# Rows of maxima copied by ScalarE's own queue, experts' weights loaded in pieces, down weights loaded two steps sooner

## The reference

```python
q = decoder_feature @ Wq.T                     # decoder_feature = layernorm(x)
k = encoder_feature @ Wk.T                     # encoder_feature = ctx_1024
v = encoder_feature @ Wv.T
att = softmax(einsum('bhtd,bhnd->bhtn', q, k) * scale, axis=-1)   # 2 * HEADS score maps
att = att[:, :, 0] - lam * att[:, :, 1]
x = x + einsum('bhtn,bhnd->bhtd', att, v)
...
scores = sigmoid(x @ gate_w.T); topk_w, topk_idx = top_k(scores, 2)
x = x + shared(x) + routed(x)                  # routed: silu(x @ gate) * (x @ up) @ down of 2 experts
```

## Time and profile before

| | |
|---|---|
| median of 3 runs | 2147.44 us (2145.28 to 2149.7) |
| the profiled execution | 2141.56 us; its span 2139.8 us |
| PE busy | 1966.6 us (92%) |
| VectorE, ScalarE, GpSimd busy | 1614.5 (75%), 1465.2 (68%), 1442.7 us (67%) |
| DMA | 432 MB, 202 GB/s over the span |
| chain that ended last | PE 58%, DMA 12%, SPq 10%, issue 8%, DVE 7% |

### The profile page before, as it was taken

One profiled execution on the slowest core, in us unless ns is written; L12 is line 12 of the kernel. 1 busy time (PEld: TensorE's weight loads), 2 busy tenths in 40 slices (PEclk: granted clock), 3 DMA queues, 4 the chain that ended last, 5 costly groups with the idle time before them and its releaser, 6 DMA issues.

```text
span 2139.8 us, 76271 instructions
## 1 busy us (share of the span) xinstructions
PE 1966.6 (92%) x20840; PEld 1417.8 (66%) x20840; DVE 1614.5 (75%) x4623; ACT 1465.2 (68%) x3511; POOL 1442.7 (67%) x2183
## 2 busy tenths in 40 slices
PE   3889999999999999999999999999888699999997
PEld 3556666666666666666666666666554599989996
DVE  2677878878878888788888787887776577767775
ACT  2577877777877778778787777787666355545553
POOL 4356767777777777777777676776655466666665
PEclk8899999999999999999999999999998699999999
DMA  4776666666666666667667666666764488868885
GB/s 125 201 205 193 189 185 204 192 191 196 199 194 195 195 195 196 194 199 198 192 198 199 183 189 194 196 198 187 210 206 174 146 263 263 260 199 275 258 268 171
DMA packets 606680, 432.00 MB, mean 202 GB/s; under 512 B 437571, under 2 KB 552394, under 8 KB 606160
## 3 DMA queue, kind: packets, MB, share of 16 engines
q1 hardware_dynamic: 545712, 319.34, 53.9%
q0 software_dynamic: 32256, 84.47, 10.8%
q10 hardware_dynamic: 28576, 26.55, 4.1%
HBM read 234.59 MB, written 197.72 MB: 202 GB/s over the span
## 4 chain that ended last, share of the span: by engine, by line
PE 58%; DMA 12%; SPq 10%; issue 8%; DVE 7%; POOL 3%; ACT 1%; DVEq 0%; POOLq 0%; ACTq 0%
PE mx_ps L491 9%; DMA stacks<-mxT 8%; PE o_ps L524 7%; SPq L369 6%; PE ms_ps L552 6%; PE ms_ps L752 5%; PE ms_ps L553 3%; PE ms_ps L554 3%; PE mx_ps L552 3%; PE mx_ps L554 3%; PE mx_ps L553 3%; PE ms_ps L573 3%; PE st_ps L730 3%; PE o_ps L535 3%; DVE mx L956 2%
## 5 line engine op out<-in xcount | busy, mean ns | idle before, releaser
L956 DVE TENSOR_REDUCE mx<-mx_ps 128x4 f32<-128x512 f32 x1024 | 696.0, 687 | 235.7 <-PE mx_ps L491 232.2
L800 ACT ACTIVATE prob<-st_ps 128x512 f32<-128x512 f32 x1024 | 607.6, 596 | 320.9 <-PE st_ps L484 306.6
L491 PE MATMUL mx_ps<-stacks 48*128 48x128 bf16 x4096 | 398.1, 221 | 88.9 <-DMA stacks<-mxT 67.1
L484 PE MATMUL st_ps<-stacks 50*128 50x128 bf16 x4096 | 396.7, 221 | 0.0
L491 PEld LDWEIGHTS mx_ps<-stacks 48*128 48x128 bf16 x4096 | 232.8, 95 | 244.3 <-issue 138.3
L524 PE MATMUL o_ps<-prob,v_sb 128*32 128x256 f32 x4096 | 332.0, 396 | 0.9 <-ACT oT L787 0.4
L1308 POOL DMA_INDIRECT rows_dram<-rowt,posi x256 | 255.0, 996 | 73.6 <-issue 63.6
L552 PE MATMUL ms_ps<-e_lo 128*128 128x256 f32 x768 | 269.6, 351 | 18.6 <-DVE rowt L1055 7.9
L484 PEld LDWEIGHTS st_ps<-stacks 50*128 50x128 bf16 x4096 | 230.6, 95 | 2.6 <-issue 1.5
L553 PE MATMUL ms_ps<-e_lo 128*128 128x256 f32 x768 | 223.1, 291 | 0.0
L554 PE MATMUL ms_ps<-e_lo 128*128 128x256 f32 x768 | 222.1, 289 | 0.0
(11 more groups left out here) (152 smaller groups left out, 4665.3 us busy)
## 6 DMA issues: line engine op xcount, KB each, us to landing
stacks<-stack_dram SPq DMA_DIRECT2D x512, 192.0 KB
stack_dram<-w_dn_sb SPq DMA_DIRECT2D x192, 256.0 KB
stacks<-rows_dram SPq DMA_DIRECT2D x288, 130.0 KB
stack_dram<-w_dn_sb SPq DMA_DIRECT2D x64, 384.0 KB
stack_dram<-w_dn_sb SPq DMA_DIRECT2D x192, 128.0 KB
w_dn_sb<-in_x SPq DMA_DIRECT2D x64, 256.0 KB
w_dn_sb<-in_ctxT SPq DMA_DIRECT2D x64, 256.0 KB
x_res<-in_x SPq DMA_DIRECT2D x64, 256.0 KB
```

The costliest lines, as they stand in the source:

```text
L484: return pe.matmul(st_ps[k % 2][:, i * P:(i + 1) * P], k_st[p][64 * h:64 * h + KROWS, u, j, :], q_st[p][64 * h:64 * h + KROWS, u, j, :], s ...
L491: return pe.matmul(mx_ps[k % 2][:, i * P:(i + 1) * P], q_st[p][64 * h:64 * h + ROWS, u, j, :], k_st[p][64 * h:64 * h + ROWS, u, j, :], sta ...
L800: nc.scalar.activation(prob[k % 4][:, :], st_ps[k % 2][:, :], ACT.Exp, scale=float(HALF) ** -0.5).then_inc(a_exp, 1)
L956: v.tensor_reduce(mx[:, u, c * CHUNK:(c + 1) * CHUNK], mx_ps[k % 2][:, :].rearrange("p (c n) -> p c n", c=CHUNK), AX.X, ALU.max).then_inc( ...
```

## The change

It has three parts. **First**, `put_max` moves from SP's program into ACT's: `copy_max` calls it right behind the copy, so ACT waits for its own copy (`a_mT`) and issues both DMAs on its own queue. SP's wait for `a_mT` and its four DMAs per turn go, and its transfers close up. **Second**, each half of the experts' gate and up weights comes in 8 transfers of one expert (256 KB) in place of one of 2 MB; the waits count 8 times as much. **Third**, the down weights come in 8 transfers of two experts (256 KB) and are issued at the head of turn 62 (`NS - 2`) in place of turn 64.

```diff
-            def put_max(s, u):
-
-                wait(sp, a_mT, 2, s, u + 1)
-                for h in range(2):
-                    row = 64 * h + ROWS
-                    sp.dma_start(q_st[s.par()][row:row + 2, u, :, :],
-                                 mxT[u][2 * SHH * h:2 * SHH * (h + 1), :]).then_inc(d_m[u], 16)
-
             def load_experts(i):
 
                 sp.wait_ge(p_st, NCH * (NS - 1 + i))
-                sp.dma_start(e_in[i], w_gu[:, i * E // 2:(i + 1) * E // 2]).then_inc(d_we[i], 16)
+                for e in range(E // 2):
+                    sp.dma_start(e_in[i][:, e], w_gu[:, i * E // 2 + e]).then_inc(d_we[i], 16)
 
             def load_down():
 
                 for read, n in ((p_xT, 1), (g_cl, 1), (g_kr, 1), (g_qs, 1), (d_qw, PW_Q), (d_kw, PW_K)):
                     sp.wait_ge(read, n * NS)
-                sp.dma_start(w_dn_sb[:, :, :], w_dn).then_inc(d_dn, 16)
+                for e in range(0, E, 2):
+                    sp.dma_start(w_dn_sb[:, e:e + 2, :], w_dn[:, e:e + 2]).then_inc(d_dn, 16)
 
             def step(it):
                 b, n2, xs = it.plus(1), it.plus(2), it.plus(4)
                 p = it.par()
+                if it.k is None and it.off == NS - 2:
+                    load_down()
                 if it.k is None and it.off in (NS - 1, NS):
                     load_experts(it.off - NS + 1)
-                    if it.off == NS:
-                        load_down()
...
                 if n2.is_in(0, NS):
                     wait(sp, g_qs, 1, n2, 1)
-                    put_parts(n2, 0, qp, d_qw, Q_RUNS[:1])
-                if it.is_in(0, NS):
-                    put_max(it, 1)
-                if n2.is_in(0, NS):
-                    put_parts(n2, 0, qp, d_qw, Q_RUNS[1:])
+                    put_parts(n2, 0, qp, d_qw, Q_RUNS)
                     wait(sp, g_ks, 1, n2, 1)
                     put_parts(n2, 1, kp, d_kw, K_RUNS)
...
                     load_stacks(n2, 0, 1)
-                if b.is_in(0, NS):
-                    put_max(b, 0)
-                if n2.is_in(0, NS):
                     load_stacks(n2, 0, 0)
...
-            pe.wait_ge(d_dn, 16)
+            pe.wait_ge(d_dn, 16 * E // 2)
...
+            def put_max(s, u):
+
+                wait(act, a_mT, 2, s, u + 1)
+                for h in range(2):
+                    row = 64 * h + ROWS
+                    act.dma_start(q_st[s.par()][row:row + 2, u, :, :],
+                                  mxT[u][2 * SHH * h:2 * SHH * (h + 1), :]).then_inc(d_m[u], 16)
+
             def copy_max(s, u):
                 wait(act, p_mT, 2, s, u + 1)
                 wait(act, d_m[u], MR, s)
                 nc.scalar.activation(mxT[u][:, :], TO.bitcast(BF16)[0:2 * SUB, 0:P], ACT.Copy).then_inc(a_mT, 1)
+                put_max(s, u)
...
-                act.wait_ge(d_we[first * 2 // E], 16)
+                act.wait_ge(d_we[first * 2 // E], 16 * E // 2)
```

## The result

The changed kernel takes 2390.38 us (median of 4 runs, 2373.51 to 2402.23) against 2148.57 us of the kernel before on the same chip (2145.28 to 2154.95): the ratio is 1.1125, 95% interval [1.1077, 1.1172]. That is 242 us slower. The forecast of 2188 us had the sign, not the size, and its range (2120 to 2240) did not hold the time.

What follows compares the result with a forecast made beforehand. PE was taken to bound the kernel, with one late transfer a turn. 54 x 0.9 - 10 x 0.6 - 2.3 = +40 us on the median of 2147.4 gave 2188 us, range 2120 to 2240.

Steps and rivals of the forecast that it cites:

- the cheap rival: Rival: if a moved issue costs ScalarE 0.38 us, a turn changes by -0.62 us, total 2097 us; chance 0.20.
- the one issuer at a time: Rival: ScalarE sits through SyncE's long issue of slot 2, 3.24 us, giving 2348 us; chance 0.03.
- The wait of slot 8: In slot 8 PE waits 0.80 us a turn for half 1's rows of maxima; forecast to go.
- part one, what it removes: On ScalarE's own queue the rows land ahead of slot 8: -0.80 us a turn; stacks late next, counted as nothing.
- rival 2, the clock: Waits of 1.4 us bring PE's 1.2 GHz clock every second turn: 46 us more, 2234 us; chance 0.20.
- that row: Trace stretch ahead of 308.1: PE busy 1.84 of 3.40 us, then 3.40 us at granted clock 0.50.
- where it lands: Slots 11 to 3: ScalarE's stretch grows from 12.39 to 14.07 us, PE waits 1.4 us; +0.9 a turn in all.
- The ring: ScalarE's stretch from slot 11 to slot 3, then PE's logits to the next slot 11: 24.89 us, +0.66.
- further knot: Slot 11's copy of the queries ends later, PE gets a bank 0.3 us late, again for slot 2: +0.25 a turn.
- turns outside the loop: Some 10 turns outside the loop's 54, where PE waits 2.3 us on the maxima: -0.6 us each.
- parts two and three: At the loop's end the scatter lands sooner, ScalarE's norm then waits for POOL: gain 2.3 us, bounds 0 and 5.4.
- The down weights' bound: Down weights go ahead of stacks that PE needs half a turn later: nothing, with 2 us as other bound.

Runs made afterwards that it cites:

- e8: The changed kernel, but SyncE waits until half 0's rows have landed before issuing the last two loads of stacks: 2278.72 us, 1.0588.
- e12: The kernel before with all experts' weights in pieces, the down weights issued where the kernel before loads them: 2149.11 us, 0.9977.
- e13: The kernel before, no transfer moved, with one extra ScalarE ACTIVATE behind the copy of the maxima in slot 11 only: 2153.59 us, 1.0015.
- e2: The kernel before with only half 1's rows (copied in slot 2) issued by ScalarE: 2217.12 us, 1.032.
- e11: As e10, with half 0's rows also on ScalarE behind slot 11's copy of the queries, and e8's wait: 2244.99 us, 1.0427.
- e5: The kernel before, no transfer moved, with one extra ScalarE ACTIVATE behind each copy of the maxima: 2255.97 us, 1.0478.
- e7: The kernel before with each two-row transfer of maxima cut into two of one row, all on SyncE's queue: 2266.57 us, 1.054.
- e1: The kernel before with only half 0's rows (copied in slot 11) issued by ScalarE: 2280.96 us, 1.0593.
- e14: As e10, with SyncE issuing half 0's rows ahead of both pairs of stacks: 2338.87 us, 1.0882.
- e6: The changed kernel with each two-row transfer of maxima cut into two of one row: 2540.26 us, 1.1801.
- e4: The kernel before with only the second and third parts: weights in pieces and down weights two turns sooner; 2158.45 us, 1.0056.
- e3: The kernel before with the first part alone: both halves' rows issued by ScalarE, end of the loop as before; 2388.47 us, 1.1106.
- e10: The kernel before with half 1's rows issued by ScalarE in slot 3, behind the copy of the values: 2130.39 us, 0.9896.

## Why the prediction was right in direction and wrong in size

**Right.** The price of an issue: 0.62 us where 0.70 was taken from SyncE's row, and not 0.38; so the cheap rival fell, and so did the one issuer at a time (a median of 0.62 leaves no room for it, and 67 of the 256 issues lie wholly inside a single issue of SyncE's, with the same median). The wait of slot 8 went. The turn of 24.23 us that the prediction read is a little short: the mean of 53 is 24.57. The gate's logits wait for the copy of the values in every turn, 1.02 us where 1.4 was forecast, and PE waits for the norm's rows by 0.28 where 0.3 was.

**Wrong, step "part one, what it removes".** "If both DMAs took as long to land as now" was worked out for half 1, whose rows left after SyncE had been held for 3.24 us, with its queue's earlier work that much further on. Half 0 was never given a landing time at all. The step named the stacks as late next and counted nothing, on the ground that SyncE issues them no later; but half 0's stacks now go as a block of three or four ahead of half 0's rows. The trace of before had 4.43 us with two loads ahead; the block made it 7.49, and 1.6 us of waiting in each turn. By e8 this one step is 1.1125 against 1.0588, some 115 of the 242 us with the clock that it brings.

**Wrong, the size of rival 2, the clock.** It stood at 0.20 and 46 us, and outside the forecast. It came, and cost 100 us or so. The runs, by the longest wait of PE that comes in most turns (for the kernel before and e12 those for rows in slots 8 and 0 together), PE's idle and busy time in a turn (mean of the 53 between the two milestones, one profiled execution each), PEclk over the loop and the ratio:

| kernel | regular wait of PE, us | idle | busy | PEclk | ratio |
|---|---|---|---|---|---|
| before | 0.96 x 46 of 55 turns | 1.13 | 23.4 | 0.99 | 1 |
| e12 | 0.99 x 54 of 55 | 1.26 | 23.5 | 0.99 | 0.9977 |
| e13 | 0.48 | 1.24 | 23.4 | 1.00 | 1.0015 |
| e2 | 1.01 | 1.56 | 24.4 | 0.96 | 1.032 |
| e11 | 0.82 x 64 in 52 turns | 2.31 | 23.9 | 0.98 | 1.0427 |
| e5 | 0.93 | 1.73 | 24.9 | 0.95 | 1.0478 |
| e7 | 1.91 | 2.21 | 24.3 | 0.95 | 1.054 |
| e8 | 1.04 | 1.94 | 24.9 | 0.95 | 1.0588 |
| e1 | 1.76 | 2.69 | 24.8 | 0.94 | 1.0593 |
| e14 | 2.23 | 2.82 | 25.0 | 0.92 | 1.0882 |
| after | 1.64 and 1.02 | 3.45 | 25.7 | 0.92 | 1.1125 |
| e6 | 2.19 and 1.50 | 4.25 | 26.7 | 0.89 | 1.1801 |

In the changed kernel +2.3 us of idle time a turn came with +2.3 us of slower work, so that it counts double. e1, e6, e7 and e14 are near that. It is no law: e2, e5 and e8 pay about three times the idle time that they add, and e11, which adds 1.2 us in smaller waits, only 1.4 times. Nor does the wait's length decide, as e12 and e2 show, near in length and far in clock. What does is not settled. "With 1.4 us idle PE would be busier than in that row" was no reason against. No run holds the clock up with the waits in place, so its share is arithmetic on PEclk and not an experiment.

**Wrong, "where it lands".** The ring had slot 11's hold travel to slot 3 through a full ScalarE. By e13 it does not get there, and by e2 slot 2's hold alone gives the whole wait for the values' copy, 1.01 us. What slot 11's hold does make is the small wait for the norm's rows that the prediction had as its further knot. The forecast of 1.4 us against 1.02 is thus near in part by luck: it was added up from both holds, and one of them makes the wait.

**Wrong, "turns outside the loop" and "parts two and three".** The ten turns were to gain 6 us; no gain is seen, and the start is 9.3 us longer and the end 6.0, neither clear of chance. The scatter's wait gave way to POOL's as forecast, but the 2.3 us for it are too few for the medians to show (e12, 0.9977 with 1 inside its interval). The down weights' bound, "nothing, with 2 us as the other", missed by 10 or more: the sentence said that they go ahead of stacks, and did not price 2 MB in front of a transfer that PE waits for. In e4 the two parts together cost 12 us.

**Still open**: why e3's +243 us is more than e1's and e2's +135 and +71 together (slot 11's hold, with no wait of slot 8 left to take it up, is the likely part, and a kernel with e2's edit and e13's would show it), and what brings the lower clock at one wait and not at another of the same length.

## What to carry to other kernels

When a small transfer that the critical path waits for leaves a queue, ask what closed up behind it: its place between large transfers was what protected it, and a queue of its own did not. Put an issue on a computing engine behind the last result that someone waits for, not directly behind the one it depends on; here two ACTIVATEs made the difference between 3.2% slower and 1.0% faster. And where TensorE is over nine tenths busy, price idle time that an edit adds in every turn at about twice its length, with 1.4 to 3.4 times as what these runs show.

## What the hardware did that I had not expected

- An issue on ScalarE whose wait is already fulfilled runs beside the ACTIVATEs in front of it: in e10 it starts at 932.39, 0.10 us after the exp started and 0.40 before the copy of the values starts, both of which stand ahead of it.
- An issue of this kind costs 0.59 to 0.61 us for one row and 0.62 to 0.70 for two: the price is one of the transfer and hardly of its size.
- Two transfers of 8 KB took 7.49 us to land behind 768 KB of another queue, 11.17 behind 2 MB and 768 KB of their own, and 4.43 with 384 KB of their own ahead of them.
- ScalarE's issues were not held up by SyncE's: 67 of ScalarE's 256 issues lie wholly inside one of SyncE's, up to 6.4 us long, and still take 0.62 us.
- The lower clock: 2 x 0.08 x 1530 = 245 us of the loop at 1.2 GHz, with PE busy for 88% of the loop.
